# Statistics of three batches moved behind the attention's first norm, zero tables set last, and maxima subtracted by VectorE

## The chip, the cores and the metric

One core of a Trainium2 chip runs the whole program. The metric is the device time of one execution in microseconds (us). Engines: TensorE (PE), VectorE (DVE), ScalarE (ACT), GpSimd (POOL), SyncE (SP); SP and POOL also issue the DMAs here, on one queue each, and 16 DMA engines carry them. PEld is TensorE's loading of weights.

## What is computed

Two layers over x of 4 batches x 512 tokens x 512 features. The change lies in the first cross attention (16 heads of 32, 64 keys) and the norm behind it.

```python
def _mha(q, k, v):                       # q = layernorm(x), k = v = ctx (4, 64, 512)
    scores = jnp.einsum('bhqd,bhkd->bhqk', qh, kh) / math.sqrt(hd)
    qi = jnp.arange(Sq)[:, None] + (Sk - Sq)
    causal = jnp.arange(Sk)[None, :] <= qi
    scores = jnp.where(causal[None, None], scores, -10000.0)
    attn = jax.nn.softmax(scores, axis=-1)
    return merge_heads(jnp.einsum('bhqk,bhkd->bhqd', attn, vh))
...
x = x + _L0_xattn_ref(_layernorm(x), ctx, ctx)
x = x + _L0_ffn_ref(_layernorm(x), ...)   # rmsnorm, latent attention, mixture of 8 experts
x = x + _L1_xattn_ref(_layernorm(x), ctx, mask)
x = x + _L1_ffn_ref(_layernorm(x), ...)   # mixture of 32 experts
```

The queries stand at positions 0 to 511 and the keys' causal offset is 64 - 512, so of each batch only the last 64 rows see a proper subset of the keys. All other rows have every score masked, their softmax is uniform, and their attention output is the plain mean of the context.

## The kernel before

Tokens lie in 16 tiles of 128 rows, 4 per batch (TPB = 4). The program is a row of blocks; all engines meet in a barrier between two blocks: cross (first cross attention), front (the FFN's attention, its router and shared expert), mixture of the first FFN, middle (second cross attention), second mixture, finish. Each engine runs its own instruction list in order and waits on semaphores. The helper hold waits and then adds to a semaphore of its own; own.run issues and waits for the result.

cross (line 326). x of batch 0 is kept in x_sb (x_first), that of batches 1 to 3 in c_x_rest. Tiles 0 to 2 of each batch need only the mean of the context: PE makes it, ACT copies it into the rows (L453), and a DMA of POOL's queue adds x from memory into it (rows_added, L420, 768 KB a batch, semaphore x_summed). Tile 3 of each batch goes through the real attention: scores on PE, then on DVE maxima(b): scale and mask (L501), add the bar (L503), reduce to the negated maximum (L504); on ACT sixteen exponentials a batch, one per head with its maximum as bias (L438); then flips (L579) and outputs (L585) on PE; on DVE totals(b) (L508, L509) and output(b): weigh (L515), add to x (L516, semaphore x_done), statistics of that tile. DVE's order: four maxima, totals 0 and 1, the wait for all four adds, statistics of batch 0's tiles, output 0, variances of batch 0 (L532), then totals, statistics and output in turn for batches 1 to 3, and the variances of the twelve other tiles (L542). Statistics of one tile are bn_stats (L474) and bn_aggr (L476).

SP in cross issues the loads, then the weights, then ten DMAs that set the routing tables and the spare rows of the two mixtures (2.8 MB in all) and a 4.2 MB field of zeros (moe_other, L392), then waits for all adds, saves tiles 0 to 2 of batches 1 to 3 into moe_sum (L396, 768 KB each), saves tile 3 of each when its x_done comes (L399), and at the end waits for weights, tables (s_init) and saves (L402).

front (line 640). POOL first clears the semaphores that cross used (27, L865), sets moe_prob (L867), on which DVE waits, and makes the second set of norms (two_norms, L319 to L323, for the 12 tiles of batches 1 to 3) from DVE's variances. DVE norms the four tiles of batch 0 (L1143, L1144), PE flips them (L1357), multiplies by the latent weights (L1421) and on; DVE comes again for the rotation (L1165). SP reloads h for batch 1 (L801), then stacks queries and keys for the scores (L793, L794). The mixture's POOL list begins with clearing the 50 semaphores in spare_front, before its table load (L1786).

Behind its reads, front's k_st takes the place in SBUF that cross's tensors had.

Of the kernel before, what the change touches and what calls it, by code (L numbers as in the profile page):

```python
# [22 lines left out]
P = 128  # L23
BATCH, SEQ, D = 4, 512, 512
TOKENS = BATCH * SEQ
TILES = TOKENS // P
TPB = SEQ // P
# [109 lines left out]
def build(nc, a, out, stop=None, debug=None):  # L137
# [8 lines left out]
    with ctx:  # L146
# [30 lines left out]
        m["x_summed"] = sem("x_summed")  # L177
# [148 lines left out]
def cross(nc, a, m, c, dram, s_init, x_first, mv, var, rstd, rms, weights):  # L326
# [5 lines left out]
    with ctx:  # L332
# [3 lines left out]
        ps, ctx_sb = m["psum"], sb("ctx_sb", [P, BATCH, D])  # L336
        GH = P // HD
        x_rest = sb("x_rest", [P, TILES - TPB, D])
# [5 lines left out]
        def x_of(b, tiles):  # L344
            return (x_first if b == 0 else x_rest[:, (b - 1) * TPB:b * TPB, :])[:, tiles, :]

        ctx_heads = sb("ctx_heads", [P, BATCH, DC, GH * KEYS])
# [7 lines left out]
        S = {n: ctx.enter_context(nc.semaphore("c_" + n)) for n in  # L355
             ("const x_q weights ones_set ctxt ctxts ctxts_act means means_out pairs var_q rstd_q xn xnt xnts s masked top e pt pts o "
              "var zeroed x_done x_saved dve pool").split()}
        x_summed, all_summed = m["x_summed"], 16 * BATCH
# [14 lines left out]
        def _(sp):  # L373
# [9 lines left out]

            for moe in (MOE0, MOE1):
# [8 lines left out]
            to = lambda b: dram["moe0"]["sum"][b * SEQ:(b + 1) * SEQ, :].rearrange("(t p) d -> p t d", p=P)  # L393
            sp.wait_ge(x_summed, all_summed)
            for b in range(1, BATCH):
                sp.dma_start(to(b)[:, 0:TPB - 1, :], x_of(b, slice(0, TPB - 1))).then_inc(S["x_saved"], 16)  # L396
            for b in range(1, BATCH):
                sp.wait_ge(S["x_done"], b + 1)
                sp.dma_start(to(b)[:, TPB - 1, :], x(b * TPB + TPB - 1)).then_inc(S["x_saved"], 16)  # L399
            sp.wait_ge(S["weights"], 16 * len(weights))  # L400
            sp.wait_ge(s_init, 16 * 10)
            sp.wait_ge(S["x_saved"], 32 * (BATCH - 1))  # L402

        @block.gpsimd
        def _(pool):
# [12 lines left out]
            def rows_added(b):  # L418
                pool.wait_ge(S["means_out"], b + 1)
                pool.dma_start(x_of(b, slice(0, TPB - 1)), x_in[:, b, 0:TPB - 1, :], accum_op=ALU.add).then_inc(x_summed, 16)  # L420
# [11 lines left out]
        def _(act):  # L432
            sc = nc.scalar

            def exponents(b):
                act.wait_ge(S["top"], b + 1)
                for h in range(HEADS):
                    ins = sc.activation(att[:, b, h, :], att[:, b, h, :], ACT.Exp, bias=neg_top[:, b, h:h + 1])  # L438
                ins.then_inc(S["e"], 1)
# [29 lines left out]
        def _(dve):  # L469
# [27 lines left out]
            def maxima(b):  # L497
# [6 lines left out]
                v.tensor_reduce(neg_top[:, b, :], att[:, b], AX.X, ALU.max, negate=True).then_inc(S["top"], 1)  # L504
# [6 lines left out]
            def output(b):  # L511
# [5 lines left out]
                hold(dve, S["x_done"], b + 1, m["passed"]["dve"])  # L517
                stats_of(x(t), t, mv[:, t, :])

            def statistics(b):  # L520
# [2201 lines left out]
```

## Time and profile before

| | us |
|---|---|
| median of 3 runs | 1736.42 |
| lowest, highest | 1733.32, 1749.18 |
| profiled execution, its own time | 1749.64 |
| its span, first to last instruction | 1747.8 |
| PE busy in it | 1509.1 (86%) |
| DVE busy | 1346.9 (77%) |
| ACT busy | 1078.9 (62%) |
| POOL busy | 765.5 (44%) |
| cross, from the start to the first norm of front | 84.05 |

The page lists busy shares, the span in slices, the DMA queues and the costliest groups. A row of the timeline gives start, duration, engine, line and operation, what it writes and reads with shapes, how many were merged into it, and in brackets the idle time of the engine before it and what ended it. A wait is put down to what came last.

### The profile page before, as it was taken

The numbers are of one execution on the slowest core, as the hardware profiler recorded it, in microseconds if no ns is written. First come the engines' busy times: TensorE is split into PE (matmuls) and PEld (weight loads), VectorE is DVE, ScalarE is ACT, GpSimd is POOL, SyncE is SP. The second block draws the span as 40 slices with busy tenths as digits, with TensorE's granted clock in tenths as the row PEclk, the third lists the DMA queues.
The fourth block names the chain that finished last, engine by engine and source line by source line (L and its number), as shares of the span: only waits on it lengthen the run. The fifth ranks groups of instructions, "written<-read, shape, count | busy, mean of one in ns | idle before, by whom it ended". The sixth has DMA issues, their size and how long they took to land. (4 is left out here: it accounts for less than half of the span.)

```text
span 1747.8 us, 34248 instructions
## 1 busy us (share of the span) xinstructions
PE 1509.1 (86%) x8728; PEld 1178.5 (67%) x8729; DVE 1346.9 (77%) x2811; ACT 1078.9 (62%) x2120; POOL 765.5 (44%) x507
## 2 busy tenths in 40 slices
PE   5378899898888989999569649999999999999990
PEld 3346667666666767777356538888887888888880
DVE  5636866866777439888377859999999999999982
ACT  6124644634545448888233238888888888888870
POOL 2100010120201324555211237888888878788881
PEclk9588998998999999999765669999999999999995
DMA  9425427344660258755645327989888898997778
GB/s 324 112 61 131 108 65 206 86 113 111 128 194 2 73 159 219 180 108 103 130 171 161 127 62 166 199 181 204 185 188 185 161 213 195 239 223 157 132 121 312
DMA packets 170175, 270.58 MB, mean 155 GB/s; under 512 B 20080, under 2 KB 95856, under 8 KB 167856
## 3 DMA queue, kind: packets, MB, share of 16 engines
q0 software_dynamic: 48048, 112.00, 33.1%
q1 hardware_dynamic: 122032, 157.43, 30.8%
q8 instruction: 46, 0.75, 0.2%
q14 instruction: 49, 0.40, 0.1%
HBM read 151.62 MB, written 91.16 MB: 139 GB/s over the span
## 5 line engine op out<-in xcount | busy, mean ns | idle before, releaser
L1793 POOL DMA_INDIRECT moe_rows<-moe_rows,moe_ids x200 | 307.2, 1536 | 66.5 <-issue 59.7
L2018 DVE TENSOR_TENSOR moe_w_lo<-moe_w_up,moe_w_hi 128x1536 fp32r<-128x1536 f32 (+1 forms) x180 | 325.8, 1810 | 1.7 <-ACT moe_w_hi L1842 1.7
L1842 ACT ACTIVATE moe_w_hi<-moe_w_up 128x1536 fp32r (+2 forms) x180 | 273.6, 1520 | 0.0
L2131 PE MATMUL psum<-moe_w_hi,moe_rows_hi 128*128 128x384 f32 (+1 forms) x720 | 262.4, 365 | 3.5 <-DVE moe_rows_lo L2012 3.5
L2132 PE MATMUL psum<-moe_w_lo,moe_rows_hi 128*128 128x384 f32 (+1 forms) x720 | 248.1, 345 | 0.0
L2133 PE MATMUL psum<-moe_w_hi,moe_rows_lo 128*128 128x384 f32 (+1 forms) x720 | 248.0, 344 | 0.0
L1804 POOL DMA_INDIRECT moe_sum<-moe_res,moe_ids x100 | 177.3, 1773 | 92.8 <-ACT moe_res L1880 50.0
L1804 POOL DMA_INDIRECT moe_other<-moe_res,moe_ids x100 | 174.1, 1741 | 83.4 <-ACT moe_res L1880 29.3
L2141 PE MATMUL psum<-moe_w_down,moe_hid_t 128*128 (+1 forms) x400 | 204.9, 594 | 0.0
L911 ACT ACTIVATE prob<-psum,neg_top 128x128 f32<-128x128 f32 (+3 forms) x256 | 133.1, 528 | 80.1 <-DVE neg_top L1101 74.6
L1101 DVE TENSOR_REDUCE neg_top<-psum 128x1 f32<-128x128 f32 (+3 forms) x256 | 117.6, 482 | 51.3 <-PE psum L1368 50.7
L2012 DVE TENSOR_TENSOR moe_rows_lo<-psum,moe_rows_hi 128x512 fp32r<-128x512 f32 x200 | 138.2, 691 | 18.1 <-ACT moe_rows_hi L1825 11.6
L300 POOL DMA_INDIRECT moe_slots<-entry,slot x32 | 33.0, 1032 | 253.2 <-DVE slot L1244 244.7
L1864 ACT ACTIVATE moe_gate<-psum 128x192 f32<-128x192 f32 (+1 forms) x200 | 68.2, 341 | 117.6 <-PE psum L2133 117.5
L2131 PEld LDWEIGHTS psum<-moe_w_hi,moe_rows_hi 128*128 128x128 f32 x720 | 135.9, 189 | 7.1 <-DVE moe_rows_lo L2012 4.3
L1409 PE MATMUL psum<-const_sb,prob 128*128 128x128 f32 x640 | 111.9, 291 | 31.7 <-ACT prob L911 28.9
L2132 PEld LDWEIGHTS psum<-moe_w_lo,moe_rows_hi 128*128 128x128 f32 x720 | 136.2, 189 | 2.8
L2133 PEld LDWEIGHTS psum<-moe_w_hi,moe_rows_lo 128*128 128x128 f32 x720 | 135.7, 188 | 3.3
L1825 ACT ACTIVATE moe_rows_hi<-psum 128x512 fp32r<-128x512 f32 x200 | 117.6, 588 | 24.3 <-PE psum L2112 23.4
L2112 PE MATMUL psum<-const_sb,moe_rows 128*128 128x128 f32 x800 | 121.4, 275 | 11.7 <-DMA moe_rows<-moe_rows,moe_ids 10.2
L2112 PEld LDWEIGHTS psum<-const_sb,moe_rows 128*128 128x128 f32 x800 | 99.8, 141 | 42.3 <-issue 8.0
L2144 PE MATMUL psum<-moe_tail_hi,moe_tail_t 128*128 128x512 f32 x160 | 127.3, 795 | 0.0
(357 smaller groups left out, 3355.2 us busy)
## 6 DMA issues: line engine op xcount, KB each, us to landing
q_st<-unit SPq DMA_DIRECT2D x128, 128.0 KB, 3.0
k_st<-unit SPq DMA_DIRECT2D x128, 128.0 KB, 3.1
moe_w_up<-in_L_ffn_w_gate SPq DMA_DIRECT2D x32, 384.0 KB
moe_w_up<-in_L_ffn_w_up SPq DMA_DIRECT2D x32, 384.0 KB
moe_w_down<-in_L_ffn_w_down SPq DMA_DIRECT2D x32, 256.0 KB
moe_w_down<-in_L_ffn_w_down SPq DMA_DIRECT2D x64, 128.0 KB
moe_sum<-x_sb SPq DMA_DIRECT2D x4, 1024.0 KB, 4.6
moe_sum<-m_x_sb SPq DMA_DIRECT2D x4, 1024.0 KB, 6.7
```

Of the source, the lines that this page charges most:

```text
L911: sc.activation(prob[:, u, e, 0:(i + 1) * P], score_at(n, e, (i + 1) * P), ACT.Exp, bias=neg_top[:, u, e:e + 1], accum_out=den[:, i, 2 * h ...
L1793: pool.indirect_dma_start(rows[u][:, :], None, d["rows"], bass.IndirectOffsetOnAxis(ids[:, t:t + 1], 0)).then_inc(gathered[u], 16)
L1804: pool.indirect_dma_start(sums[t % 2], bass.IndirectOffsetOnAxis(ids[:, t:t + 1], 0), res[t % RESULTS][:, :], None, compute_op=ALU.add).th ...
L1842: sc.activation(w_hi[u % SPLITS][:, :], up_of(at), ACT.Copy).then_inc(T["wh"], 1)
L2012: v.tensor_tensor(rows_lo[i][:, :], ps[:, i, :], rows_hi[i][:, :].bitcast(F32), ALU.subtract).then_inc(T["rts"], 1)
L2018: v.tensor_tensor(w_lo[u % SPLITS][:, :], up_of(at), w_hi[u % SPLITS][:, :].bitcast(F32), ALU.subtract).then_inc(T["wl"], 1)
L2112: last = tr(ps[:, i, k * P:(k + 1) * P], rows[u][:, k * P:(k + 1) * P], ident)
L2131: mm(ps[:, 2 + i, 0:2 * I], hi, w_h, start=(k == 0), stop=False)
L2132: mm(ps[:, 2 + i, 0:2 * I], hi, w_l, start=False, stop=False)
L2133: last = mm(ps[:, 2 + i, 0:2 * I], lo, w_h, start=False, stop=(k == DC - 1))
L2141: mm(ps[:, 5 + i, :], hid_t[i][:, j, :], tile_at(w_down, at * n_fc + j), start=(j == 0), stop=False)
L2144: mm(ps[:, 5 + i, :], tail_t[i][:, :], tail_hi[u][:, :], start=False, stop=False)
```

## The change

In maxima(b) DVE adds the negated maxima to the scores, and ACT takes one exponential over the whole 128x1024. In DVE's list of cross only the statistics of batch 0 stay; it waits only for the add of batch 0 (x_summed is two semaphores now). The statistics of the other twelve tiles and their variances are made by DVE in front, behind the four norms of batch 0 and before the first rotation; for this c_x_rest lies outside the space that front's first tensors use, and SP waits for the new semaphore var before it stacks keys into that space, as POOL does before the second set of norms. SP issues the saves of tiles 0 to 2 ahead of the tables, and its waits for tables and saves move from the end of cross into front, ahead of the reload of h. In front POOL sets moe_prob first and clears cross's semaphores after it. The shared expert's semaphores are no longer taken from cross's, and eight more, and var, are cleared at the start of the mixture.

```diff
@@ -174,7 +174,8 @@
...
         m["listed0"] = sem("listed0")
-        m["x_summed"] = sem("x_summed")
+        m["scattered0"] = sem("scattered0")
+        m["x_summed"], m["x_saved"] = [sem("x_summed_first"), sem("x_summed_rest")], sem("x_saved")
         m["passed"] = {e: sem(f"passed_{e}") for e in ("dve", "pool", "pe", "act", "sp")}
@@ -323,7 +324,7 @@
...
-def cross(nc, a, m, c, dram, s_init, x_first, mv, var, rstd, rms, weights):
+def cross(nc, outer, a, m, c, dram, s_init, x_first, mv, var, rstd, rms, weights):
@@ -333,9 +334,12 @@
...
-        ps, ctx_sb = m["psum"], sb("ctx_sb", [P, BATCH, D])
+        ps = m["psum"]
         GH = P // HD
-        x_rest = sb("x_rest", [P, TILES - TPB, D])
+        ctx_heads = sb("ctx_heads", [P, BATCH, DC, GH * KEYS])
+        x_rest = m["x_rest"] = nc.alloc_sbuf_tensor_at("x_rest", [P, TILES - TPB, D], F32, offset=nc.sbuf_base)
+        sb("rows_room", [P, TILES - TPB, D])
+        ctx_sb = sb("ctx_sb", [P, BATCH, D])
@@ -344,7 +348,6 @@
...
-        ctx_heads = sb("ctx_heads", [P, BATCH, DC, GH * KEYS])
         ctx_pairs = sb("ctx_pairs", [P, BATCH, HEADS // 2, 2 * HD])
@@ -352,10 +355,10 @@
...
         att_t = sb("att_t", [P, BATCH, HEADS // 2, P])
-        S = {n: ctx.enter_context(nc.semaphore("c_" + n)) for n in
+        S = {n: outer.enter_context(nc.semaphore("c_" + n)) for n in
              ("const x_q weights ones_set ctxt ctxts ctxts_act means means_out pairs var_q rstd_q xn xnt xnts s masked top e pt pts o "
-              "var zeroed x_done x_saved dve pool").split()}
-        x_summed, all_summed = m["x_summed"], 16 * BATCH
+              "var zeroed x_done dve pool").split()}
+        x_summed, x_saved, rest_summed = m["x_summed"], m["x_saved"], 16 * (BATCH - 1)
         x_in = a["x"].rearrange("b (t p) d -> p b t d", p=P)
@@ -381,6 +384,10 @@
...
+            to = lambda b: dram["moe0"]["sum"][b * SEQ:(b + 1) * SEQ, :].rearrange("(t p) d -> p t d", p=P)
+            sp.wait_ge(x_summed[1], rest_summed)
+            for b in range(1, BATCH):
+                sp.dma_start(to(b)[:, 0:TPB - 1, :], x_of(b, slice(0, TPB - 1))).then_inc(x_saved, 16)
             for moe in (MOE0, MOE1):
@@ -390,16 +397,10 @@
...
             sp.dma_start(dram["moe1"]["other"][0:TOKENS, :].rearrange("(n p) d -> n (p d)", p=P), zeros).then_inc(s_init, 16)
-            to = lambda b: dram["moe0"]["sum"][b * SEQ:(b + 1) * SEQ, :].rearrange("(t p) d -> p t d", p=P)
-            sp.wait_ge(x_summed, all_summed)
-            for b in range(1, BATCH):
-                sp.dma_start(to(b)[:, 0:TPB - 1, :], x_of(b, slice(0, TPB - 1))).then_inc(S["x_saved"], 16)
             for b in range(1, BATCH):
                 sp.wait_ge(S["x_done"], b + 1)
-                sp.dma_start(to(b)[:, TPB - 1, :], x(b * TPB + TPB - 1)).then_inc(S["x_saved"], 16)
+                sp.dma_start(to(b)[:, TPB - 1, :], x(b * TPB + TPB - 1)).then_inc(x_saved, 16)
             sp.wait_ge(S["weights"], 16 * len(weights))
-            sp.wait_ge(s_init, 16 * 10)
-            sp.wait_ge(S["x_saved"], 32 * (BATCH - 1))
@@ -417,7 +418,7 @@
...
                 pool.wait_ge(S["means_out"], b + 1)
-                pool.dma_start(x_of(b, slice(0, TPB - 1)), x_in[:, b, 0:TPB - 1, :], accum_op=ALU.add).then_inc(x_summed, 16)
+                pool.dma_start(x_of(b, slice(0, TPB - 1)), x_in[:, b, 0:TPB - 1, :], accum_op=ALU.add).then_inc(x_summed[min(b, 1)], 16)
@@ -434,9 +435,7 @@
...
                 act.wait_ge(S["top"], b + 1)
-                for h in range(HEADS):
-                    ins = sc.activation(att[:, b, h, :], att[:, b, h, :], ACT.Exp, bias=neg_top[:, b, h:h + 1])
-                ins.then_inc(S["e"], 1)
+                sc.activation(att[:, b], att[:, b], ACT.Exp).then_inc(S["e"], 1)
@@ -501,7 +500,8 @@
...
                 own.run(v.tensor_tensor(att[:, b], att[:, b], c["barred"].unsqueeze(1).to_broadcast([P, HEADS, KEYS]), ALU.add))
-                v.tensor_reduce(neg_top[:, b, :], att[:, b], AX.X, ALU.max, negate=True).then_inc(S["top"], 1)
+                own.run(v.tensor_reduce(neg_top[:, b, :], att[:, b], AX.X, ALU.max, negate=True))
+                v.tensor_tensor(att[:, b], att[:, b], neg_top[:, b, :].unsqueeze(2).to_broadcast([P, HEADS, KEYS]), ALU.add).then_inc(S["top"], 1)
@@ -514,32 +514,24 @@
...
                 v.tensor_tensor(x(t), x(t), xn[:, b, :], ALU.add).then_inc(S["x_done"], 1)
-                hold(dve, S["x_done"], b + 1, m["passed"]["dve"])
-                stats_of(x(t), t, mv[:, t, :])
-
-            def statistics(b):
-                for t in range(b * TPB, b * TPB + TPB - 1):
-                    stats_of(x(t), t, mv[:, t, :])
...
             totals(1)
-            dve.wait_ge(x_summed, all_summed)
-            statistics(0)
+            dve.wait_ge(x_summed[0], 16)
+            for t in range(TPB - 1):
+                stats_of(x(t), t, mv[:, t, :])
             output(0)
+            hold(dve, S["x_done"], 1, m["passed"]["dve"])
+            stats_of(x(TPB - 1), TPB - 1, mv[:, TPB - 1, :])
             own.wait()
...
             totals(2)
-            statistics(1)
             output(1)
             totals(3)
-            statistics(2)
             output(2)
-            statistics(3)
             output(3)
-            own.wait()
-            own.run(v.tensor_scalar(var[:, TPB:TILES], mv[:, TPB:TILES, 1], EPS, None, ALU.add))
@@ -660,7 +652,7 @@
...
-        cross(nc, a, m, c, dram, s_init, x, mv, var, rstd, rms, [
+        cross(nc, ctx, a, m, c, dram, s_init, x, mv, var, rstd, rms, [
             (w_kvd[:, :, :], a["L0_ffn_kv_d_w"].rearrange("(c p) n -> p c n", p=P)),
@@ -710,14 +702,15 @@
...
-        names = ("scales z zt zts kvd qd kvds qds pp pr pv_ qkp qkr vs tq tk qts kts qls kls x_in x_back st ntop pexp pt pta ptb pv rden rdt rdts "
+        names = ("scales var z zt zts kvd qd kvds qds pp pr pv_ qkp qkr vs tq tk qts kts qls kls x_in x_back st ntop pexp pt pta ptb pv rden rdt rdts "
                  "attd hres acc oproj var2 rms2 hn hnt hnts logit lgs lge masked ranked slotted scattered sent rows_out dve").split()
-        S = {n: sem("f_" + n) for n in names}
+        S = {n: sem("f_" + n) for n in names if n != "scattered"} | {"scattered": m["scattered0"]}
         light_in, heavy_in = [sem(f"f_light{k}") for k in range(DC)], [sem(f"f_heavy{k}") for k in range(DC)]
-        m["spare_front"] = [s for n, s in S.items() if n != "scattered"]
-        sh = m["shared"] = {n: m["early"].enter_context(nc.semaphore("sh_" + n, num=m["spare_cross"].pop().num)) for n in SHARED_NAMES}
+        m["spare_front"] = [s for n, s in S.items() if n != "scattered"] + light_in + heavy_in
+        sh = m["shared"] = {n: m["early"].enter_context(nc.semaphore("sh_" + n)) for n in SHARED_NAMES}
         over = lambda name, shape, dt, at: nc.alloc_sbuf_tensor_at("o_" + name, shape, dt, offset=at)
         chunks = lambda t: [t[:, k, :] for k in range(t.shape[1])]
+        x_rest = m["x_rest"]
         SIZE = 4 * DC * SEQ
@@ -797,10 +790,13 @@
...
+            sp.wait_ge(s_init, 16 * 10)
+            sp.wait_ge(m["x_saved"], 32 * (BATCH - 1))
             sp.wait_ge(S["zt"], TPB)
...
             sp.wait_ge(S["kls"], 2)
+            sp.wait_ge(S["var"], 1)
             for k in range(DC):
@@ -862,11 +858,12 @@
...
             g = nc.gpsimd
+            g.memset(r["prob"][:, :, :], -1.0).then_inc(S["scales"], 1)
+            pool.sem_inc(S["sent"], 1)
             for used in m["spare"]:
                 pool.sem_clear(used)
-            g.memset(r["prob"][:, :, :], -1.0).then_inc(S["scales"], 1)
-            pool.sem_inc(S["sent"], 1)
             own = Steps(pool, S["scales"], 1)
+            pool.wait_ge(S["var"], 1)
             two_norms(g, own, m, var, mv, rstd, rms, slice(TPB, TILES)).then_inc(S["scales"], 1)
@@ -1290,6 +1287,12 @@
...
                 normed(0, t)
+            for n in range(TPB, TILES):
+                own.did(v.bn_stats(stats[:, n % TPB, :], x_rest[:, n - TPB, :]))
+                own.hold()
+                own.did(v.bn_aggr(mv[:, n, :], stats[:, n % TPB, :]))
+            own.wait()
+            v.tensor_scalar(var[:, TPB:TILES], mv[:, TPB:TILES, 1], EPS, None, ALU.add).then_inc(S["var"], 1)
             for t in range(TPB):
...
                 if t >= 1:
```

## Rows read from the trace of the kernel before

**Rows 1.** Waits of the engines, 0 to 140 us: total, times, longest.

```profile
DVE c_stats L474 <- DMA c_x_rest<-in_x: 9.8, 1, 9.8
```

**Rows 2.** Timeline, maxima on DVE and exponentials on ACT.

```profile
28.11 1.23 DVE L501 SCALAR_TENSOR_TENSOR c_att<-psum,const_sb 128x1024 f32<-128x1024 f32 x1 [3.76 <-PE psum L569]
29.48 1.23 DVE L503 TENSOR_TENSOR c_att<-c_att,const_sb 128x1024 f32<-128x1024 f32 x1
31.88 1.21 DVE L501 SCALAR_TENSOR_TENSOR c_att<-psum,const_sb 128x1024 f32<-128x1024 f32 x1
45.38 3.92 ACT L438 ACTIVATE c_att<-c_att,c_neg_top 128x64 f32<-128x64 f32 x16
```

**Rows 3.** Timeline, DVE, statistics and output of batch 1.

```profile
63.34 0.70 DVE L474 BATCH_NORM_STATS2 c_stats<-c_x_rest 128x6 f32<-128x512 f32 x1
66.09 0.66 DVE L515 TENSOR_TENSOR c_xn<-psum,c_total 128x512 f32<-128x512 f32 x1
68.56 1.19 DVE L508 TENSOR_REDUCE c_total<-c_att 128x16 f32<-128x1024 f32 x1
```

**Rows 4.** Timeline, last save, first norm, second set of norms.

```profile
79.41 0.32 SPq L399 DMA_DIRECT2D moe_sum<-c_x_rest  x1
84.05 0.55 DVE L1143 TENSOR_SCALAR h<-x_sb,mv,rstd 128x512 f32<-128x512 f32 x1 [3.29 <-POOL moe_prob L867]
88.26 2.56 POOL L323 TENSOR_TENSOR rms<-rms,power 128x12 f32<-128x12 f32 x1
```

**Rows 5.** Timeline, first rotation and first stacking DMA.

```profile
105.62 0.69 DVE L1165 TENSOR_TENSOR rot_a<-psum,const_sb 128x512 f32<-128x512 f32 x1 [16.14 <-PE psum L1437]
121.47 0.69 SPq L793 DMA_DIRECT2D q_st<-unit  x1
```

**Rows 6.** Timeline, PE, outputs and first products.

```profile
47.44 3.51 PE L585 MATMUL psum<-c_ctx_pairs,c_att_t 128*128 128x64 f32 x16
52.45 4.04 PE L585 MATMUL psum<-c_ctx_pairs,c_att_t 128*128 128x64 f32 x32
91.34 10.21 PE L1421 MATMUL psum<-z_t,shared_up 128*128 128x512 f32 x16 [0.69 <-ACT z_t L924]
```

**Rows 7.** DMA, queues of 15 to 56, of 37 to 42 (packets, MB, share); one issue.

```profile
q0 software_dynamic: 1600, 3.15, 42.1%
...
q1 hardware_dynamic: 18, 1.18, 67.2%
q0 software_dynamic: 16, 0.03, 3.5%
...
x_sb<-in_x POOLq DMA_DIRECT2D x1, 768.0 KB, 14.5
```

**Rows 8.** Waits of SP's queue, 0 to 125 and 604 to 640 us.

```profile
SPq L402 <- DMA moe_sum<-c_x_rest: 1.7, 1, 1.7
SPq L860 <- DMA moe_other<-o_res: 4.4, 1, 4.4
```

**Rows 9.** Timeline, change of block into the first mixture.

```profile
628.10 0.36 SPq L850 DMA_DIRECT2D moe_other<-o_res  x1
633.44 0.38 SPq L1623 DMA_DIRECT2D moe_w_up<-in_L_ffn_r_gate  x1
636.72 0.14 DVE L1969 COPY moe_pair<-moe_begun 128x1 f32<-128x1 f32 x1
637.66 1.00 POOL L1786 DMA_INDIRECT moe_table<-moe_slots,moe_block  x1 [26.46 <-DVE moe_pair L1969]
646.77 0.66 PE L2112 MATMUL psum<-const_sb,moe_rows 128*128 128x128 f32 x4 [0.68 <-DMA moe_rows<-moe_rows,moe_ids]
```

**Rows 10.** Windows: us, busy and count by engine, clock, DMA share, GB/s.

```profile
57.00:58.00 1.00, 0.00 (x0) 0.00 (x0) 0.85 (x4) 0.00 (x0) 0.00 (x0) 1.00 1.02 377
91.00:98.00 7.00, 6.66 (x9) 2.81 (x10) 0.00 (x0) 0.28 (x1) 0.00 (x0) 0.53 0.47 150
128.00:142.00 14.00, 9.06 (x40) 7.57 (x40) 8.24 (x18) 4.74 (x14) 0.00 (x0) 0.51 0.85 194
```

## The prediction

> **What bounds the kernel now.** The page comes first: PE is busy 86% of the span and DVE 77%, averages that say nothing of the first 100 us, where the diff lies. So I asked what ended each idle time in the first 140 us. DVE waits 9.8 us for the DMA that adds x into c_x_rest [rows 1]. Around that wait the timeline shows one serial chain on DVE: maxima of four batches from 28.11 on, totals, statistics and outputs in turn, the end of the block, and the first norm at 84.05, before which DVE waited 3.29 us for POOL's memset of moe_prob [rows 2 to 4]. Everything behind waits for that norm. After the norms DVE sits idle for 16.14 us, until PE brings it the first rotation at 105.62 [rows 5]. I therefore forecast the start of the first norm, and ask then whether later work keeps what is gained.
>
> **Maxima subtracted by DVE: 5.0 us onto the path.** One addition over 128x1024 per batch goes in behind the reduce. The nearest row is L503, the same shape and engine: 1.23 us; with the hand-over 1.26 [rows 2]. The maximum is broadcast along the keys instead of the rows; L515 broadcasts in that way over half the elements in 0.66 us [rows 3], no dearer per element. 4 x 1.26 = 5.0; bounds 4 x 1.2 and 4 x 1.4. The period of a batch goes from 31.88 - 28.11 = 3.77 to 5.03; maxima end at 28.11 + 4 x 5.03 = 48.2.
>
> **One exponential for sixteen: off the path.** Sixteen took 3.92 us [rows 2]; one over the same elements takes no more and not under nothing. At either end ACT has batch 4 ready by 48.2 + 3.9 = 52.1, and PE flips it after 54. DVE does not wait for ACT here, so the saving is worth nothing. The question is whether PE stays ahead of DVE. PE resumes once the fourth batch is masked, 28.11 + 3 x 5.03 + 1.2 = 44.4. At the low clock flips and outputs of a batch repeat every 52.45 - 47.44 = 5.0 us [rows 6]; the four outputs end near 49.7, 54.7, 59.7 and 63, the last near 60 if the clock rises as it did before (two outputs in 4.04 [rows 6]). DVE comes for them at 54.0, 58.5, 61.5, 62.9. Cost 0, at worst 0.3.
>
> **The wait for the adds: 9.8 us gone.** DVE now waits for the add into batch 0 alone, which landed 14.5 us after its issue at 17.9, so by 33; DVE comes for it at 51.3. The four adds need 42.1% of 41 us = 17.3 us of all 16 DMA engines. They were late because the zero tables went ahead: from 37 to 42 us the adds had 3.5% of the engines, the other queue 67.2% for 18 packets and 1.18 MB [rows 7]. Free of them they end near 22 + 17.3 = 40. (The Trainium skill, "DMA: Bandwidth & Descriptors", section Queues, rings and completion order, has each DMA engine take turns between queues packet by packet; the row with 18 large packets agrees. By that rule the sum is the same.)
>
> **Statistics moved out: 10.4 us.** Three tiles of a batch take 66.09 - 63.34 = 2.75 us, three times: 8.2. The last tile of a batch: from the output's first instruction to the next work 68.56 - 66.09 = 2.47 us, of which the two output instructions are 1.39; 1.08 saved, for batches 1 and 2 [rows 3]. That of batch 3 ran in the shadow of SP's wait and counts nothing. SP issued the last save at 79.41 [rows 4]; new: 79.4 + 5.0 - 9.8 - 10.4 = 64.2.
>
> **The end of the block.** From that issue to the first norm were 84.05 - 79.41 = 4.64 us: 0.32 of issue [rows 4], 1.7 until it landed [rows 8], the barrier, 27 semaphores cleared by POOL, the memset. The landing and the clears now lie behind the start. The barrier I take from the next change of block: issue ended at 628.46, 4.4 us of landing, next issue at 633.44 [rows 8, 9], so 0.6. For the clears 4.64 - 0.32 - 1.7 - 0.6 - 0.2 (memset, hand-over) = 1.8 is left, 0.07 each. New first norm: 64.2 + 0.3 + 0.6 + 0.2 = 65.3, **18.7 us earlier**. Bound: if the clears were free and the barrier takes those 1.8 too, 16.9.
>
> **What comes back in the next block.** Twelve statistics (2.75 / 3 = 0.92 each: 11.0) and one small operation go behind four norms of 1.4 us each. They end near 65.3 + 5.5 + 11.2 = 82.0; the rotation is due at 105.62 - 18.7 = 86.9. Cost 0, with 5 us to spare; without this cover 11 us. POOL's second set of norms took from 84.02 to 90.8 [rows 4]; it ends near 89, before the stacking DMAs due at 121.47 - 18.7 = 102.8 [rows 5], and its reader comes later still. SP: three saves (2.4 MB) at 40, then ten table DMAs (2.8 MB, and 4.2 MB of zeros) by 48; 9.4 MB at the 377 GB/s of the saves [rows 10] is 25 us, all landed by 67. SP now waits for this, and for the variances (82), ahead of the first stacking DMA at 102.8: 20 us to spare. The three late saves queue behind tables, and the barrier no longer waits for them. Cost 0.
>
> **Nine more clears: 0.6 us lost.** At the start of the first mixture block POOL clears 59 semaphores instead of 50 before its first gather. Its issue at 637.66 comes 0.8 us after the value it waits for (636.72 + 0.14), so the clears seem to set it; the table leads to rows for which PE waited 0.68 us at 646.77 [rows 9]. 9 x 0.07 = 0.6; bounds 0 and 0.65.
>
> **The sum.** -18.7 + 0.6 = -18.1 us; bounds of the terms -15.7 and -18.9. On the profiled execution (1749.64 us; its span 1747.8 and 1.8 around it) that gives 1731.5. The median of the runs shown is 13.2 us less, 1736.42. None of the durations above belongs to that difference by the rows, so the same 18.1 comes off: **1718.3 us**.
>
> **TensorE's clock.** PE had no work from 56.5 [rows 6] until the first norm was out, and in 91 to 98 its granted clock averages 0.53 (nearly all at 1.2 GHz, risen to 2.4 at the end) although PE is busy for 6.66 of the 7 us; the sixteen products of L1421 take 10.21 [rows 6, 10]. Now PE pauses some 6 us, not 29. Were the clock up all through L1421, the 6.2 us at the low level would take half: 3.1 saved; if it rises that much later, as much is lost. I take 0: the row shows that work alone does not bring the clock back at once. (The Trainium skill, "TensorE: Matmul & The Clock Gate", section What's actually happening, says that the moment of the change varies from run to run, since its window runs freely. One trace cannot show that.)
>
> **Rivals.**
> A. The clock stays up over the short pause. For it the pause, against it 91 to 98 as above. 1718.3 - 3.1 = 1715.2 us.
> B. The gain is given back later: a shifted start moves the low spells of the clock. One like that of 128 to 142, with 9.06 us of PE work in it [rows 10], costs up to 7 us in a stage where PE never rests, two cost 14. For it: three runs of this kernel lie 16 us apart (1733.32 to 1749.18). Against: no step of the change makes such spells more. 1725 to 1732 us.
> C. The block's end is dearer than read (barrier 2.4, or SP's issues slowed by the tables in its queue): 2 us. 1720.3 us.
> D. The other side: the tables land late and hold the stacking DMAs. Up to 102.8 it costs nothing, then each microsecond counts once: at 121.5 the gain is gone, at 139 the kernel is slower by 1%, 1754 us. From 40 on, that takes the tables 99 us instead of the 27 worked out.
>
> **How the numbers follow.** Forecast (the terms' bounds and some 3 us of clock and spread: 1713 to 1723) 0.67; A 0.10; B 0.13; C 0.07; D 0.03. From 1710, a little under A, to 1731, nearly all of B, less than 2 in 10 is left out. About 1% (17.4 us) is what a measurement of this kernel can tell from no change, and 18.1 stands almost on that edge: of the 0.67, 0.41 go to faster; with A 0.51. The rest, B and C are 0.46 within 1%; D 0.03 slower.
>
> **What would show each step.** In the changed profile: 5.0 us between the L501 of two batches, no idle of DVE before its first statistics; the last output ended near 64; the first norm near 65.3; twelve statistics over before 83 and some 5 us of idle left before the rotation; the first stacking DMA near 103. Wrong if the first norm starts after 68, if DVE waits for PE at an output, if PE waits for the rotation, or if all this is as said and the end is not 18 us earlier.

## The result and the profile after

The changed kernel runs at **0.9907 of the time before, 95% interval 0.988 to 0.9933** (20 runs of each): 0.9% less, about 16 us (12 to 21 by the interval). The forecast, 18.1 us of 1736.42, is a ratio of 0.9896 and lies inside the interval. The medians are 1732.09 us (1716.48 to 1747.19) against 1740.28 (1732.68 to 1761.4), only 8.2 us apart. The ratio leaves disturbed runs out, which the medians take in, and that is a part of the difference: without its two longest runs (1747.19 and 1746.1) the changed kernel's median is 1729.63. As a time, the forecast was missed: 1718.3 us with 1713 to 1723 around it, where the median is 1732.09. The kernel before also came out at 1740.28 over twenty runs instead of the 1736.42 that the forecast started from. The profiled execution took 1741.89 us (span 1740.1) against the 1749.64 (span 1747.8) of before: only 7.8 us less. Where the rest of the forecast's 18.1 went in this one execution is read below.

| first 110 us | before | forecast | after |
|---|---|---|---|
| first maximum's L501 (after: L500) starts | 28.11 | 28.11 | 28.54 |
| period of a batch of maxima | 3.77 | 5.03 | 5.02 |
| DVE waits for the adds | 9.8 | 0 | 0 |
| first norm starts | 84.05 | 65.3 | 65.71 |
| from L501 or L500 to the first norm | 55.94 | 37.2 | 37.17 |
| the twelve statistics over | (in the block before) | before 83 | 82.24 |
| DVE's idle before the first rotation | 16.14 | 5 | 4.17 |
| first stacking DMA | 121.47 | 102.8 | 102.25 |

Timeline of the changed kernel on DVE and ACT: start, duration, engine and line, operation, shapes; in brackets the idle time before and what ended it. These rows answer [rows 2 to 5]. Here and below, rows that nothing is read from are left out.

```profile
28.54 1.23 DVE L500 SCALAR_TENSOR_TENSOR c_att<-psum,const_sb 128x1024 f32<-128x1024 f32 x1 [3.73 <-PE psum L561]
...
32.42 1.22 DVE L504 TENSOR_TENSOR c_att<-c_att,c_neg_top 128x1024 f32<-128x1024 f32 x1
33.56 1.22 DVE L500 SCALAR_TENSOR_TENSOR c_att<-psum,const_sb 128x1024 f32<-128x1024 f32 x1
33.68 1.06 ACT L438 ACTIVATE c_att<-c_att 128x1024 f32<-128x1024 f32 x1 [3.71 <-DVE c_att L504]
...
51.41 0.25 DVE L509 RECIPROCAL c_total<-c_total 128x16 f32<-128x16 f32 x1
51.70 0.69 DVE L473 BATCH_NORM_STATS2 c_stats<-x_sb 128x6 f32<-128x512 f32 x1
53.86 0.18 DVE L475 BATCH_NORM_AGGREGATE mv<-c_stats 128x2 f32<-128x6 f32 x1 [0.57 <-DVE c_stats L473]
...
63.98 0.69 DVE L516 TENSOR_TENSOR x_rest<-x_rest,c_xn 128x512 f32<-128x512 f32 x1
65.71 0.55 DVE L1140 TENSOR_SCALAR h<-x_sb,mv,rstd 128x512 f32<-128x512 f32 x1 [1.03 <-POOL moe_prob L861]
...
82.07 0.17 DVE L1295 TENSOR_SCALAR var<-mv 128x12 f32<-128x12 f32 x1
...
86.42 0.69 DVE L1162 TENSOR_TENSOR rot_a<-psum,const_sb 128x512 f32<-128x512 f32 x1 [4.17 <-PE psum L1440]
```

The addition, L504, takes 1.22 us and the batch repeats after 5.02. The one exponential takes 1.06 us where sixteen took 3.92. Nothing is in brackets before the statistics at 51.70: the wait for the adds is gone. The last output starts at 63.98 and the first norm follows at 65.71. Ahead of the rotation DVE is still idle for 4.17 us, so the twelve statistics ended in time.

SP's queue and POOL, same kernel:

```profile
37.55 2.02 SPq L390 DMA_DIRECT2D moe_sum<-x_rest  x3
39.62 1.36 SPq L393 DMA_DIRECT2D moe_slots<-in_moe_empty  x1
...
47.67 1.39 SPq L399 DMA_DIRECT2D moe_other<-in_zero_rows  x1
...
60.51 4.51 SPq L402 DMA_DIRECT2D moe_sum<-x_rest  x3
65.55 0.12 POOL L861 MEMSET moe_prob<- 128x32 f32 x1 [4.88 <-POOLq L333]
...
85.53 2.27 POOL L324 TENSOR_TENSOR rms<-rms,power 128x12 f32<-128x12 f32 x1
102.25 0.69 SPq L786 DMA_DIRECT2D q_st<-unit  x1
...
618.00 0.39 SPq L1626 DMA_DIRECT2D moe_w_up<-in_L_ffn_r_gate  x1
622.86 1.43 POOL L1789 DMA_INDIRECT moe_table<-moe_slots,moe_block  x1 [27.09 <-issue]
```

The last save's issue ends at 60.51 + 4.51 = 65.02 and the memset starts at 65.55: the barrier between the blocks costs 0.53 us, and from the end of that issue to the first norm are 0.69 us, where 84.05 - 79.41 - 0.32 = 4.3 were [rows 4]. POOL's second set of norms is over at 87.8. At the first mixture the table's load comes 4.86 us behind SP's first weights, against 637.66 - 633.44 = 4.22 before [rows 9]: 0.64 us for nine more clears.

**Where the profiled execution lost it.** Both kernels issue the same number of matmuls from the attention on, so the k-th from the end of one can be set against the k-th from the end of the other. Lead over the profiled execution of before, in us, at times of before (the second mixture's matmuls start near 1100):

| kernel | 84 | 350 | 520 | 650 | 880 | 1000 | 1100 | 1300 | 1600 |
|---|---|---|---|---|---|---|---|---|---|
| changed | 18.3 | 17.2 | 13.6 | 11.4 | 14.0 | 18.3 | 19.8 | 9.1 | 7.1 |
| changed, again (e10) | 17.5 | 23.4 | 14.3 | 8.9 | 11.4 | 15.9 | 17.6 | 17.6 | 15.8 |
| tables first (e3) | 16.9 | 21.4 | 20.7 | 16.0 | 18.5 | 24.5 | 25.6 | 25.6 | 36.1 |
| waits at the end (e5) | 12.0 | 16.3 | 15.6 | 9.7 | 12.3 | 12.2 | 12.2 | 12.2 | 22.6 |

At 1100 us the changed kernel still leads by 19.8; by 1600 it has lost 12.7 of it, in code that the change does not touch. Windows over the first 200 us of that stage, before and after (start and end, length, busy time and count of PE, PEld, DVE, ACT, POOL, granted clock, DMA share, GB/s):

```profile
1100.00:1300.00 200.00, 200.00 (x1077) 168.32 (x1076) 195.37 (x343) 174.41 (x295) 167.58 (x97) 1.00 0.87 193
```

```profile
1080.00:1291.00 211.00, 202.29 (x1080) 168.06 (x1079) 195.39 (x345) 176.19 (x295) 167.77 (x99) 1.00 0.85 187
```

And the waits of the changed kernel in that stretch (total us, times, longest us):

```profile
POOL moe_sum L1807 <- DMA moe_sum<-moe_res,moe_ids: 8.2, 3, 3.1
PE psum L2115 <- DMA moe_rows<-moe_rows,moe_ids: 7.9, 6, 1.7
```

The same 1077 to 1080 matmuls lasted 200 us before and 211 after; the clock is 1.00 in both, PE's own work 202 against 200. The difference is idle time: PE waited 7.9 us for gathered rows, and POOL, which issues those gathers, 8.2 us for its scatters to land. The table's other rows say that this is no property of the changed code: the same code again (e10) loses nothing from 1100 to 1300, and e3 gains 10.5 us from 1300 to 1600. The same pattern stands in other traces that lose there: in e2, e6 and e12 the stretch lasts 207, 205 and 206 us, and PE waits 5.3, 4.0 and 5.1 us for gathered rows. Over 1100 to 1600 the profiled executions of the changed kernel and of e1 to e12 range from 12.7 us longer than before to 10.5 us shorter.

### The profile page after: what moved, and what is told of

It is laid out like the page before. It is cut to its first block and busy times, and to the rows that moved or that the text cites. A ratio compares the mean times of both kernels' runs of the same rounds, so it can differ in the third digit from the quotient of the medians.

```text
span 1740.1 us, 34198 instructions
## 1 busy us (share of the span) xinstructions
PE 1504.5 (86%) x8728; PEld 1170.1 (67%) x8729; DVE 1351.7 (78%) x2815; ACT 1070.4 (62%) x2060; POOL 765.0 (44%) x507
## 5 line engine op out<-in xcount | busy, mean ns | idle before, releaser
L1796 POOL DMA_INDIRECT moe_rows<-moe_rows,moe_ids x200 | 281.8, 1409 | 66.1 <-issue 59.1
L1807 POOL DMA_INDIRECT moe_sum<-moe_res,moe_ids x100 | 189.2, 1892 | 104.1 <-ACT moe_res L1883 50.1
L1807 POOL DMA_INDIRECT moe_other<-moe_res,moe_ids x100 | 187.7, 1877 | 83.5 <-ACT moe_res L1883 33.7
L2115 PEld LDWEIGHTS psum<-const_sb,moe_rows 128*128 128x128 f32 x800 | 97.9, 140 | 56.2 <-issue 17.5
```

Of the source, the lines that this page charges most:

```text
L1796: pool.indirect_dma_start(rows[u][:, :], None, d["rows"], bass.IndirectOffsetOnAxis(ids[:, t:t + 1], 0)).then_inc(gathered[u], 16)
L1807: pool.indirect_dma_start(sums[t % 2], bass.IndirectOffsetOnAxis(ids[:, t:t + 1], 0), res[t % RESULTS][:, :], None, compute_op=ALU.add).th ...
L2115: last = tr(ps[:, i, k * P:(k + 1) * P], rows[u][:, k * P:(k + 1) * P], ident)
```

## The experiments

Each kernel computes the whole result. Several of them ran once only. Since single times of one kernel lie up to 37 us apart (e3: 1698.64 to 1735.34), what is read of them is the distance from the first maximum (L500 or the line that took its place) to the first norm: **37.17 us in the changed kernel, 55.94 before**. It repeats to 0.02 us (37.17 in e3, e7 and e10, 37.16 in e8).

**Each part by itself**

e1, the kernel before with the subtraction alone:

```diff
-                for h in range(HEADS):
-                    ins = sc.activation(att[:, b, h, :], att[:, b, h, :], ACT.Exp, bias=neg_top[:, b, h:h + 1])
-                ins.then_inc(S["e"], 1)
+                sc.activation(att[:, b], att[:, b], ACT.Exp).then_inc(S["e"], 1)
...
+                v.tensor_tensor(att[:, b], att[:, b], neg_top[:, b, :].unsqueeze(2).to_broadcast([P, HEADS, KEYS]), ALU.add).then_inc(S["top"], 1)
```

> The kernel before with one part of the change alone: DVE subtracts the maxima, ACT takes one exponential per batch. Theory (the opening is DVE's chain, and here the chain waits for the adds until 56.0): the 5.0 us of additions vanish in the 9.8 us of waiting, the wait shrinks to about 4.8, and the first norm stays at 84.0 within 0.5. Rival (an addition costs its length wherever it stands): first norm at 89. Rival (ACT's shorter exponentials pay): first norm earlier than 83.

Timeline of e1, DVE:

```profile
28.39 1.22 DVE L499 SCALAR_TENSOR_TENSOR c_att<-psum,const_sb 128x1024 f32<-128x1024 f32 x1 [4.09 <-PE psum L568]
...
56.12 0.69 DVE L472 BATCH_NORM_STATS2 c_stats<-x_sb 128x6 f32<-128x512 f32 x1 [4.61 <-DMA c_x_rest<-in_x]
...
84.20 0.55 DVE L1142 TENSOR_SCALAR h<-x_sb,mv,rstd 128x512 f32<-128x512 f32 x1 [3.30 <-POOL moe_prob L866]
```

While DVE still waits for all the adds, the four additions go into that wait: it shrinks from 9.8 to 4.61 us and the first norm starts at 84.20 (before 84.05). The kernel took 1738.85 us, before 1739.52. So the 5.0 us are a price only together with the wait's end, as the sum had it: +5.0 - 9.8.

e2, the changed kernel with e1's lines turned round (sixteen exponentials, no subtraction). 

> The changed kernel with this part undone: sixteen exponentials per batch with the maximum as bias, no subtraction by DVE. Theory (DVE's chain sets the first norm and PE keeps ahead of it): first norm 5.0 us earlier than in the changed kernel, 65.7 - 5.0 = 60.7, and about 0.3% less time than the changed kernel, 1.2% less than before. Rival (then ACT, with 3.9 + 1.1 us a batch, or PE behind it is the bound): first norm 62 to 66, DVE idle in front of an output.

```profile
29.25 1.22 DVE L502 SCALAR_TENSOR_TENSOR c_att<-psum,const_sb 128x1024 f32<-128x1024 f32 x1 [5.28 <-PE psum L562]
...
61.33 0.55 DVE L1141 TENSOR_SCALAR h<-x_sb,mv,rstd 128x512 f32<-128x512 f32 x1 [1.03 <-POOL moe_prob L862]
```

61.33 - 29.25 = 32.08: 5.09 us less than in the changed kernel. The subtraction is a loss of 5 us at the first norm. The ratio to before is 0.9897 (0.981 to 0.9985), too wide to show 5 us; e11 takes it up.

e4, the statistics of batches 1 to 3 back in cross attention:

```diff
+            def statistics(b):
+                for t in range(b * TPB, b * TPB + TPB - 1):
+                    stats_of(x(t), t, mv[:, t, :])
...
-            for n in range(TPB, TILES):
-                own.did(v.bn_stats(stats[:, n % TPB, :], x_rest[:, n - TPB, :]))
```

> The changed kernel with the statistics of batches 1 to 3 made in the first block again, between the outputs, waiting for the other three adds once. Theory: these adds have landed by 40, so no wait; 10.4 us of statistics come back onto the chain and 0.9 us of the last pair beyond SP's last issue: first norm at 65.7 + 11.3 = 77.0, and the idle time before the first rotation grows from 4.2 to about 15. Rival (the wait comes back with them): idle of DVE before batch 1's statistics, first norm at 80 or later.

```profile
78.52 0.55 DVE L1152 TENSOR_SCALAR h<-x_sb,mv,rstd 128x512 f32<-128x512 f32 x1 [0.74 <-POOL moe_prob L874]
...
99.20 0.69 DVE L1174 TENSOR_TENSOR rot_a<-psum,const_sb 128x512 f32<-128x512 f32 x1 [15.23 <-PE psum L1446]
```

The first maximum started at 29.85, so the distance is 48.67: 11.50 us more. That is the forecast's 10.4 and the 1.1 of batch 3, which lay in SP's shadow before and does not here. DVE's idle before the rotation is 15.23 again, so it was this idle time that took them. The kernel took 1746.18 us (before 1739.52).

**The order of SP's queue**

e3, the zero tables ahead of the first three saves, as before the change:

```diff
-            sp.wait_ge(x_summed[1], rest_summed)
-            for b in range(1, BATCH):
-                sp.dma_start(to(b)[:, 0:TPB - 1, :], x_of(b, slice(0, TPB - 1))).then_inc(x_saved, 16)
...
```

> The changed kernel with SP issuing the tables ahead of the saves again, as before. Theory (what removed the wait is that DVE waits for batch 0's add alone; the order of the tables is off the path): first norm 65.7 within 0.5, the adds of batches 1 to 3 land near 56 again, and the time is that of the changed kernel. Rival (the tables' order removed the wait): batch 0's add or the saves come late and the first norm is 3 us or more later.

```profile
29.93 1.22 DVE L500 SCALAR_TENSOR_TENSOR c_att<-psum,const_sb 128x1024 f32<-128x1024 f32 x1 [5.07 <-PE psum L561]
...
58.40 2.03 SPq L399 DMA_DIRECT2D moe_sum<-x_rest  x3
...
67.10 0.55 DVE L1140 TENSOR_SCALAR h<-x_sb,mv,rstd 128x512 f32<-128x512 f32 x1 [1.03 <-POOL moe_prob L861]
```

67.10 - 29.93 = 37.17, the changed kernel's to the hundredth, although the adds and with them the saves came 20 us later (58.40 against 37.55). The first norm itself comes at 67.10 and not at 65.7, because the first maximum began 1.4 us later. Ratio 0.9911 (0.9846 to 0.9977). So the zero tables set last earn nothing here: once DVE waits for batch 0's add alone, nobody on the path asks for the others, and the second semaphore by itself takes the 9.8 us away. The reverse was not run, but the changed kernel's rows answer it: SP's first saves wait for the adds of batches 1 to 3 and are issued at 37.55, and DVE comes for the statistics at 51.70. With the tables last, one semaphore for all four adds would have held nobody either. (In e4 DVE asks for all four adds, and no idle time stands before the statistics of batch 1.) Either step alone removes the wait.

e5, SP's waits for tables and saves back at the end of cross attention:

```diff
             sp.wait_ge(S["weights"], 16 * len(weights))
+            sp.wait_ge(s_init, 16 * 10)
+            sp.wait_ge(x_saved, 32 * (BATCH - 1))
```

> The changed kernel with SP's waits for tables and saves back at the end of the first block; the tables stay last. In the changed kernel the first norm starts 37.2 us after the first scaling of scores (L500). Theory (the tables, 9.4 MB with the saves at 377 GB/s from 37.6 on, land near 63 to 66, and the last save 2 us after its issue at 64.7): the barrier comes 1.7 to 2 us later, 39 us from L500 to the first norm. Rival D (the tables land late): 42 us or more; the landing time can be read from SP's wait.

```profile
SPq L405 <- DMA moe_sum<-x_rest: 6.1, 1, 6.1
...
72.02 0.55 DVE L1140 TENSOR_SCALAR h<-x_sb,mv,rstd 128x512 f32<-128x512 f32 x1 [7.14 <-POOL moe_prob L861]
```

With the first maximum at 28.74 the distance is 43.28: 6.1 us more, all of it SP's wait. I had put the landing at 1.7 to 2, as it was before [rows 8].

e9, e3 and e5 together, to ask what made it 6.1. 

> The changed kernel with the zero tables ahead of the first three saves AND SyncE's waits for tables and saves back at the end of cross attention. With the tables last, moving those waits back cost 6.1 us, where I had taken 1.7 to 2. Theory: the last save sat behind the tables' large packets in the same queue; with the tables long landed only the other saves are ahead of it, SyncE waits 2 to 3 us at the end of the block, and the first norm comes 39.2 to 40.2 us after the last maximum's line begins (37.17 in the changed kernel, 43.28 with tables last and waits at the end). Rival: a 256 KB save issued at the end of the block needs its 6 us to land whatever is ahead of it: wait about 6, first norm at 43. About 1735 us.

The wait, the first maximum, the first norm and the time from issue to landing of the last saves in e9, then that time in e5:

```profile
SPq L405 <- DMA moe_sum<-x_rest: 1.7, 1, 1.7
...
29.63 1.22 DVE L502 SCALAR_TENSOR_TENSOR c_att<-psum,const_sb 128x1024 f32<-128x1024 f32 x1 [5.25 <-PE psum L563]
...
68.50 0.55 DVE L1140 TENSOR_SCALAR h<-x_sb,mv,rstd 128x512 f32<-128x512 f32 x1 [2.73 <-POOL moe_prob L861]
...
moe_sum<-x_rest SPq DMA_DIRECT2D x3, 256.0 KB, 2.0
```

```profile
moe_sum<-x_rest SPq DMA_DIRECT2D x3, 256.0 KB, 6.4
```

With the tables landed first the wait is 1.7 us again and the distance 38.87, 1.70 more than in the changed kernel (I had expected 2 to 3 us of wait and 39.2 to 40.2). The rival, that such a save needs its 6 us anyway, falls. Such a 256 KB save lands 2.0 us after its issue with only the other saves ahead of it, and 6.4 us with the tables ahead (medians of the three saves). (The Trainium skill, "DMA: Bandwidth & Descriptors", section Queues, rings and completion order, has each DMA engine take up the descriptors of one queue in their order; the two rows agree.) So the moved wait is worth 1.7 us with the tables first and 6.1 with the tables last: the tables' new place would have cost 4.4 us by itself had the wait stayed, and costs nothing only because it went.

**The clears**

e6, cross attention's 26 clears ahead of the memset again. 

> The changed kernel with POOL clearing the first block's 26 semaphores before the memset again. Theory (0.07 to 0.08 us each): first norm 1.8 to 2.1 us later, 39.0 to 39.3 us after L500 instead of 37.2. Rival (the clears are free and the barrier took the time before): 37.2 as in the changed kernel.

```profile
67.47 0.55 DVE L1140 TENSOR_SCALAR h<-x_sb,mv,rstd 128x512 f32<-128x512 f32 x1 [2.89 <-POOL moe_prob L863]
```

The first maximum started at 28.45: distance 39.02, 1.85 us more, 0.071 us a clear. The forecast had 1.8 and 0.07.

e7, the 59 clears of the front moved behind the first mixture's first gathers. 

> The changed kernel with the 59 clears at the start of the first mixture moved behind POOL's first gathers. In the changed kernel POOL's table load starts 4.86 us after SP's first issue of that block, 1.4 us after DVE's value is there. Theory (the clears hold it): it starts 3.7 to 3.9 us after SP's issue, and the stage is about 1 us shorter. Rival (POOL waits for DVE alone): 4.86 as before. The 1 us can not be seen in the whole time.

```profile
612.25 0.39 SPq L1626 DMA_DIRECT2D moe_w_up<-in_L_ffn_r_gate  x1
...
615.57 1.00 POOL L1786 DMA_INDIRECT moe_table<-moe_slots,moe_block  x1 [24.99 <-DVE moe_block L1968]
...
622.12 0.97 POOL L1793 DMA_INDIRECT moe_rows<-moe_rows,moe_ids  x1 [5.55 <-DVE moe_ids L1986]
```

The table's load comes 3.32 us behind SP's mark (its issue at 612.25), 1.54 earlier than in the changed kernel and earlier than the 3.7 to 3.9 expected, and now waits for DVE's value instead of POOL's own work. But the first gather comes 9.87 us behind the mark against 628.41 - 618.00 = 10.41: of 1.54 us, 0.54 is left, because the table's rows pass through DVE before the gather, and not the 1 us that I had expected. The kernel before, with 50 clears in that place, has 643.30 - 633.44 = 9.86: those 50 cost the gather nothing. The other traces with 59 clears have 10.11 to 10.49. The nine more clears (0.64 at the load) are therefore worth 0.3 to 0.6 where it matters.

**The cover of the statistics**

e8, the twelve statistics made twice; the second pass writes the same values:

```diff
-            for n in range(TPB, TILES):
+            for n in 2 * list(range(TPB, TILES)):
```

> The changed kernel with the twelve statistics of the second block made twice over (same values written again): 10.9 us more for DVE between the norms and the first rotation, where the changed kernel leaves 4.2 us idle. Theory (the cover is what is idle, and beyond it each microsecond counts once): no idle before the rotation, which starts 10.9 - 4.2 = 6.7 us later, 27.4 us after the first norm instead of 20.7, and the first stacking DMA 5 to 7 us later, 41.5 to 43.2 us after the first norm instead of 36.5. Rival (the next waits of this stage absorb it): stacking within 2 us of 36.5.

DVE of e8, then PE of e8, then PE of the changed kernel at the same instructions:

```profile
94.26 0.69 DVE L1162 TENSOR_TENSOR rot_a<-psum,const_sb 128x512 f32<-128x512 f32 x1
...
96.46 1.22 PE L1438 MATMUL psum<-shared_down,q_d 128*128 128x256 f32 x2 [5.51 <-DVE qk L1169]
97.47 3.33 PE L1440 MATMUL psum<-shared_up,z_t 128*128 128x256 f32 x8
...
100.84 0.69 DVE L1162 TENSOR_TENSOR rot_a<-psum,const_sb 128x512 f32<-128x512 f32 x1 [4.44 <-PE psum L1440]
```

```profile
88.95 0.59 PE L1438 MATMUL psum<-shared_down,q_d 128*128 128x256 f32 x2
89.38 1.89 PE L1440 MATMUL psum<-shared_up,z_t 128*128 128x256 f32 x8
```

The first norm started at 66.95. The first rotation now starts 27.31 us behind it, with no idle time before it, against 20.71 in the changed kernel: 10.9 us more work, 4.2 of it in the idle time, and the rest on the path. (The same distance varies between traces of one code: it is 21.40 in e10. Against that, 5.9 us are on the path.) PE then waits 5.51 us for the rotated tile, and comes back at half the clock: the same products of L1440 take 3.33 us instead of 1.89 (the granted clock is 0.50 from 94 to 98 and 1.00 from 86 to 95 in the changed kernel). The first stacking DMA comes 44.8 us behind the first norm against 36.5 (37.2 in e10): 8.3 us, or 7.6 against e10, where I had expected 5.0 to 6.7. From the rotation to that DMA are 17.5 us, in every other trace 15.8 or 15.9; I put these 1.7 us down to the low clock. The pause of PE has a price of its own.

**Does it reach the end?**

e10 to e12 ran on one chip beside the same 11 runs of before (median 1742.44 us), six runs of each: the changed kernel, e2's kernel, and e2's with e7's late clears.

> The changed kernel as it is, timed on the chip and beside the same runs of the kernel before as the next two. The forecast's theory: 18.7 us earlier at the first norm, less 0.6 for the clears, ratio to before 0.987 to 0.993. Rival, that much of the lead is given back in the second mixture and in spells of low clock whatever the code: 0.993 to 1.0 here, and the order of the three kernels of this call is arbitrary.

> The changed kernel with the sixteen exponentials of ScalarE and no subtraction by VectorE. Theory: the first norm 5.1 us earlier than in the changed kernel (32.1 us after the last maximum's line begins, against 37.2), and nothing downstream takes it back, so 4 to 6 us less than the changed kernel, ratio to before 0.984 to 0.989. Rival: it is lost in the spread of the later stages, and the time is within 2 us of the changed kernel's.

> The sixteen exponentials back, and the 59 semaphores' clears moved behind the first mixture's first gathers. Theory: 5.1 us from the exponentials and 0.5 from the clears (the gather came 9.87 us after SyncE's mark against 10.41), so 5 to 6.5 us less than the changed kernel, ratio to before 0.983 to 0.989, the fastest of the three though not to be told from the one with early clears. Rival: the spread of the later stages is larger than this, and the three lie within 2 us of each other.

| kernel | to the first norm | median | lowest to highest | ratio to before (95%) |
|---|---|---|---|---|
| e10 changed | 37.17 | 1727.02 | 1720.77 to 1734.21 | 0.9869 (0.9816 to 0.9923) |
| e11 sixteen exponentials | 32.10 | 1725.45 | 1720.37 to 1729.45 | 0.9873 (0.9819 to 0.9926) |
| e12 and late clears | 32.10 | 1727.74 | 1714.57 to 1739.82 | 0.9876 (0.9813 to 0.9939) |

The gain of the change is there again: 1.3% by the ratio, 0.9% by the medians (1727.02 against 1742.44). The three medians lie within 2.3 us of each other, as the rival said, and e12, which I had expected to be the fastest, has the highest. This doesn't show that the 5.1 us are lost: an interval of half a per cent either way is 9 us. In the profiled executions e11 leads e10 by 5.7 us at the first norm, by 5.1 at 880 us and by 3.5 at 1200. That the sixteen exponentials make the kernel faster at its end stays open, and so does which of the three is the fastest.

## Why the prediction was right, and where it was not

- **The chain and what bounds it.** The forecast took DVE's chain up to the first norm for the bound. Forecast distance 65.3 - 28.11 = 37.2, measured 37.17; 18.8 us gained against 18.7. PE's lead at 84 us is 18.3. That much is shown. That the end is 18 us earlier is not shown as closely: the ratio's interval is 12 to 21 us, and the medians differ by 8.2 us here and by 15.4 in e10.
- **Four additions, 5.0.** Period 5.02, and 5.09 by e2. Right.
- **One exponential, 0.** PE never made DVE wait at an output. Right.
- **The adds, 9.8.** No wait. Right in size. The forecast named the separate semaphore and the tables' place together and priced them as one; e3 shows that the semaphore is enough by itself, and the saves' issue at 37.55 that the tables' place would be too.
- **The statistics, 10.4.** e4 gives 11.50, of which 1.1 is batch 3's, which the forecast rightly left out. An idle of 0.57 us at 53.86, inside batch 0's statistics, was not foreseen. It is there in every kernel that subtracts, and not in before, e2, e11 and e12, which don't and have an idle of 0.27 at the first output instead; why was not tried.
- **The end of the block, 3.5.** Barrier 0.53 (0.6), clears 1.85 (1.8). The landing taken out, 1.7, is right against before [rows 8]. **The mis-sized number is the landing in the new order**: "all landed by 67" had the last save fall in with the tables at 377 GB/s. It landed about 71: its issue ended at 65.22 in e5 and SP waited another 6.1 us. The rate did not hold to the end either: e5's DMAs moved 212 GB/s from 64 to 67 and 145 from 67 to 70. Since nothing waits for it until 102.8, the sum did not change.
- **The cover, 5 us to spare.** 4.17 left, and 3.41 to 4.94 in the ten traces with the twelve statistics in that place; it moves with the time that PE's first products take (the clock, below). Past the cover the price is a little over one for one (e8).
- **Nine more clears, 0.6.** 0.64 at the load, 0.3 to 0.6 at the gather behind it (e7).
- **The clock, 0.** Right, as far as the traces tell. In the profiled execution PE's first products took 9.34 us where they had taken 10.21 [rows 6]; so the rotation came 20.71 us behind the first norm instead of 105.62 - 84.05 = 21.57, and PE's lead grows from 18.3 at 84 us to 19.2 at 105. It looks like rival A: the pause of PE had shrunk from 28.95 to 6.59 us. But the clock still started low (0.50 from 66 to 70), and the other traces say that it is spread: the same code again (e10) took 10.03 after 5.93 us of pause, e1 only 8.75 after 25.05. Over all fourteen traces the products took 8.57 to 10.21 us, in no order by the pause before them. PE's first instruction behind the norm, before, then PE of the changed kernel, of e10 and of e1:

```profile
85.44 1.12 PE L1357 MATMUL psum<-const_sb,h 128*128 128x128 f32 x4 [28.95 <-DVE h L1144]
```

```profile
67.10 1.12 PE L1360 MATMUL psum<-const_sb,h 128*128 128x128 f32 x4 [6.59 <-DVE h L1141]
...
73.00 9.34 PE L1424 MATMUL psum<-z_t,shared_up 128*128 128x512 f32 x16 [0.69 <-ACT z_t L921]
```

```profile
67.94 1.12 PE L1360 MATMUL psum<-const_sb,h 128*128 128x128 f32 x4 [5.93 <-DVE h L1141]
...
73.84 10.03 PE L1424 MATMUL psum<-z_t,shared_up 128*128 128x512 f32 x16 [0.69 <-ACT z_t L921]
```

```profile
85.59 1.12 PE L1356 MATMUL psum<-const_sb,h 128*128 128x128 f32 x4 [25.05 <-DVE h L1143]
...
91.50 8.75 PE L1420 MATMUL psum<-z_t,shared_up 128*128 128x512 f32 x16 [0.69 <-ACT z_t L923]
```

- **Rival B** (gain given back later) is what the one profiled execution shows: 12.7 us, but by waits for gathered rows and scatters at full clock in the second mixture, not by the low clock that I named, and not again in e10. Low clock moves the lead too: between 350 and 520 us of before e10 takes 178.8 us for the same 1215 matmuls (169.7 before) at a clock of 0.91 (0.94 before), after a stretch in which it had won 5.9 us at 0.95 (0.93 before). By the ratios nothing is given back, 0.9907 and 0.9869 agree with the forecast's 0.9896 within their intervals; but the median of 1732.09 is at rival B's 1725 to 1732, and the medians' 8.2 us leave room for a part of it.
- **Rival C**: the barrier was no dearer. **Rival D**: the tables did land later than worked out, by some 4 us, and still 31 us ahead of the stacking DMA.

## What to carry to other kernels

Price an edit as a distance between two instructions on the path, here from the first maximum to the first norm. That distance repeats to hundredths where the whole time scatters by 1%, and it tells apart what timing cannot. A distance that holds a stretch of PE at a changing clock does not: from the first norm to the first rotation it is 19.94 to 21.57 us in thirteen traces, so a difference of 0.9 us between two of them shows nothing. When several edits come together, ask of each what it is worth with the others in place: the subtraction was free while DVE waited anyway and costs 5.1 us now, the tables' order earns nothing once the wait is split (and splitting it would earn nothing once the tables go last), and a moved wait is worth 1.7 or 6.1 us by what stands ahead of it in the queue. Work that is put off belongs where its engine has a measured idle time, and it should leave some of it: beyond it the next engine stands still too and may come back at half the clock.

## What the runs showed of the hardware

- A 256 KB save landed 2.0 us after its issue with other saves ahead of it in the queue and 6.4 us with the zero tables ahead (medians of three, e9 and e5).
- Semaphores cleared by POOL cost 0.071 us each, 1.85 us for 26 (e6); the barrier between two blocks took 0.53 us.
- The second mixture, untouched and at full clock, differed by up to 23 us between profiled executions: where it is longer, PE waits for gathered rows while POOL waits for scatters into moe_sum to land (7.9 and 8.2 us in the changed kernel, 4.0 and 5.5 in e6, none and 0.8 in e10). What makes it one or the other was not tried.
- After a pause of 5.5 us in the midst of its work PE ran the same eight products in 3.33 us instead of 1.89 (e8).
- Behind the barrier PE's first sixteen products took 8.57 to 10.21 us over fourteen traces, in no order by the pause before them (4.77 to 28.95 us).
